# Cross attention in a decoder layer: where the head outputs are divided by their softmax sums

## The reference

```
x = x + self_attention(layernorm(x))                 # 2 x 256 tokens, width 128, 16 heads of 64
x = x + cross_attention(layernorm(x), ctx, ctx, mask) # 16 heads of 8, 512 keys
x = x + ffn(layernorm(x))                             # shared expert and 8 experts, best 2 of 8
```

## Time and profile before

| what | us |
| --- | --- |
| median of 3 runs | 205.86 (205.72 to 267.74) |
| the profiled execution | 205.74 |
| span of its profile, first to last instruction | 203.9 |
| TensorE busy in the span | 192.7 (94%) |
| VectorE busy | 157.2 (77%) |
| ScalarE busy | 138.0 (68%) |
| GpSimd busy | 96.6 (47%) |

### The profile page before, as it was taken

The page is one execution under the profiler, slowest core; times in us unless marked ns, Lnnn a source line. Parts: engine busy times, 40 slices in busy tenths (PEclk is TensorE's granted clock), DMA queues, the critical chain, the costliest instruction groups (busy, mean ns, idle before and its releaser), DMA issues.

```text
span 203.9 us, 4609 instructions
## 1 busy us (share of the span) xinstructions
PE 192.7 (94%) x1626; PEld 151.2 (74%) x1626; DVE 157.2 (77%) x418; ACT 138.0 (68%) x318; POOL 96.6 (47%) x145
## 2 busy tenths in 40 slices
PE   7999998999999699996999999999989999999995
PEld 7688776777877467764666657575568799999994
DVE  2579989668868677679999999999973866458844
ACT  2599879669766939189998898987986332452220
POOL 7599127588458835806669991003300017500430
PEclk9999999999999889999999999999999999999999
DMA  6970407604555015579844100000000000000001
GB/s 159 385 217 3 154 2 244 225 2 59 59 62 58 2 39 119 73 90 119 94 117 111 21 2 0 5 0 3 0 0 3 5 0 0 3 0 13 3 0 39
DMA packets 13301, 12.69 MB, mean 62 GB/s; under 512 B 1072, under 2 KB 11312, under 8 KB 13280
## 3 DMA queue, kind: packets, MB, share of 16 engines
q1 hardware_dynamic: 12176, 11.15, 26.7%
q10 hardware_dynamic: 1008, 1.06, 1.6%
q0 software_dynamic: 96, 0.20, 0.5%
HBM read 10.96 MB, written 1.44 MB: 61 GB/s over the span
## 4 chain that ended last, share of the span: by engine, by line
PE 75%; DVE 9%; ACT 7%; issue 3%; POOL 2%; DMA 1%; DVEq 0%; POOLq 0%
PE ps L985 13%; PE ps L944 9%; PE ps L886 8%; PE ps L870 8%; PE ps L1009 8%; PE ps L754 6%; PE ps L921 5%; PE ps L842 5%; PE ps L903 4%; PE ps L767 4%; ACT q_t L669 3%; ACT prob L635 2%; DVE q_t L1215 2%; DMA x_in<-in_x 1%; DVE prob_t L1323 1%
## 5 line engine op out<-in xcount | busy, mean ns | idle before, releaser
L509 POOL TENSOR_TENSOR prob<-prob,rec 128x512 f32<-128x512 f32 x32 | 32.7, 1047 | 24.2 <-DVE rec L1274 24.2
L1215 DVE CUSTOM_DVE_ANT_0 q_t<-ps,mask_add 128x512 f32<-128x512 f32 x64 | 41.4, 685 | 3.4 <-PE ps L903 2.2
L635 ACT ACTIVATE prob<-ps,low 128x256 f32<-128x256 f32 x64 | 29.7, 489 | 7.3 <-DVE low L1205 7.3
L669 ACT ACTIVATE q_t<-q_t,low 128x512 f32<-128x512 f32 x44 | 29.4, 719 | 4.2 <-DVE low L1215 4.1
L944 PEld LDWEIGHTS ps<-ident,q_t 128*128 128x128 f32 x176 | 19.6, 141 | 8.7 <-ACT q_t L669 2.9
L1205 DVE TENSOR_REDUCE low<-ps 128x2 f32<-128x512 f32 x32 | 20.5, 684 | 7.2 <-PE ps L842 7.1
L944 PE MATMUL ps<-ident,q_t 128*128 128x128 f32 x176 | 23.7, 276 | 2.1 <-ACT place_k L707 0.8
L548 POOL TENSOR_TENSOR place_k<-place_k 128x256 f32<-128x256 f32 x10 | 7.3, 733 | 38.7 <-DVE place_k L1240 38.7
L655 ACT ACTIVATE q_t<-ps 128x512 f32<-128x512 f32 x18 | 10.6, 599 | 21.1 <-PE ps L985 21.0
L886 PE MATMUL ps<-ident,prob 128*128 128x128 f32 x128 | 19.0, 283 | 2.7 <-ACT prob_t L643 1.4
L1261 DVE TENSOR_TENSOR q_t<-q_t,ps 128x512 f32<-128x512 f32 x18 | 12.2, 684 | 11.4 <-PE ps L985 8.2
(11 more groups left out here) (183 smaller groups left out, 470.7 us busy)
## 6 DMA issues: line engine op xcount, KB each, us to landing
k_stack<-k_dram SPq DMA_DIRECT2D x18, 128.0 KB
wg<-in_L_ffn_w_gate SPq DMA_DIRECT2D x1, 1024.0 KB, 5.4
wu<-in_L_ffn_w_up SPq DMA_DIRECT2D x1, 1024.0 KB, 8.0
q_stack<-q_dram SPq DMA_DIRECT2D x6, 144.0 KB
k_dram<-prob SPq DMA_DIRECT2D x1, 768.0 KB, 3.6
w_in<-in_L_attn_Wq ACTq DMA_DIRECT2D x2, 256.0 KB, 5.5
context<-in_ctx SPq DMA_DIRECT2D x1, 512.0 KB, 5.7
w_in<-in_L_attn_Wv SPq DMA_DIRECT2D x1, 512.0 KB, 7.3
```

The source lines that it names most:

```text
L509: nc.gpsimd.tensor_tensor(pr, pr, rec1[:, s % 2, r, :].unsqueeze(2).to_broadcast([P, C, S]), ALU.mult).then_inc(s_norm1, 1)
L635: e = nc.scalar.activation(prob1[:, s % 3, r, c * S:(c + 1) * S], ps[:, 2 * (s % 2) + r, c * S:(c + 1) * S], ACT.Exp, bias=low1[:, s % 2, ...
L669: nc.scalar.activation(prob2[n % 3][:, c, :], score2[n % 2][:, c, :], ACT.Exp, bias=low2[:, n % 2, c:c + 1], scale=-1.0).then_inc(s_exp2, 1)
L1215: nc.vector.tensor_tensor_reduce(out=score2[n % 2][:, c, :], in0=ps[:, 2 * (n % 2) + c, :], in1=mask_add[:, c, :], scale=1.0, scalar=3e38, ...
```

## The change

VectorE no longer divides. ScalarE copies the transposed outputs with their sums (72 of the 256 columns) out of PSUM to `o_sum` in SBUF, between `exp2(n)` and the copy of the second half of `turn2(n-2)`. GpSimd raises the sums to the power -1 and multiplies. `values2(k+1)` now waits for ScalarE's copy (`s_osum`) and no longer for the division.

```diff
+        o_sum = sb("o_sum", [P, C, HG, HD2 + 1])
+        minus_one = sb("minus_one", [P, C, HG])
...
             link(nc.gpsimd.memset(minus_half[:, :], -0.5))
+            nc.gpsimd.memset(minus_one[:, :, :], -1.0)
...
@@ GpSimd, step n, after the norms, before split_weights
+                if n in O_READY:
+                    k = O_READY[n]
+                    b, hg = divmod(k, NG)
+                    pool.wait_ge(s_osum, k + 1)
+                    link(nc.gpsimd.tensor_tensor(rec2[:, :, :], o_sum[:, :, :, HD2], minus_one[:, :, :], ALU.pow))
+                    nc.gpsimd.tensor_tensor(
+                        o2[:, b * C:(b + 1) * C, hg * HG * HD2:(hg + 1) * HG * HD2].rearrange("p c (g d) -> p c g d", g=HG),
+                        o_sum[:, :, :, 0:HD2], rec2[:, :, :].unsqueeze(3).to_broadcast([P, C, HG, HD2]), ALU.mult
+                        ).then_inc(s_o2, 1)
                 if 0 <= n - SPLIT_N < 2 * (NE + 1):
                     split_weights(n - SPLIT_N)
@@ ScalarE, step n
                 if 0 <= n < N_CROSS:
                     exp2(n)
+                if n in O_READY:
+                    k = O_READY[n]
+                    act.wait_ge(s_oturn, k + 1)
+                    if k >= 1:
+                        act.wait_ge(s_o2, k)
+                    nc.scalar.copy(o_sum[:, :, :, :], ps[:, O2_BANK[k], S:2 * S].rearrange(
+                        "p (c g d) -> p c g d", c=C, g=HG)[:, :, :, 0:HD2 + 1]).then_inc(s_osum, 1)
@@ TensorE, values2
-                        pe.wait_ge(s_o2, k)
+                        pe.wait_ge(s_osum, k)
@@ VectorE, step n
-                if n in O_READY:
-
-                    k = O_READY[n]
-                    b, hg = divmod(k, NG)
-                    dve.wait_ge(s_oturn, k + 1)
-                    o = ps[:, O2_BANK[k], S:2 * S].rearrange("p (c g d) -> p c g d", c=C, g=HG)
-                    link(nc.vector.reciprocal(rec2[:, :, :], o[:, :, :, HD2]))
-                    nc.vector.tensor_tensor(
-                        o2[:, b * C:(b + 1) * C, hg * HG * HD2:(hg + 1) * HG * HD2].rearrange("p c (g d) -> p c g d", g=HG),
-                        o[:, :, :, 0:HD2], rec2[:, :, :].unsqueeze(3).to_broadcast([P, C, HG, HD2]), ALU.mult
-                        ).then_inc(s_o2, 1)
```

More of the change, by code:

```diff
@@ L324, in build @@
         s_turn2a, s_turn2b, s_pt2a, s_pt2b = map(sem, ("s_turn2a", "s_turn2b", "s_pt2a", "s_pt2b"))
-        s_pv2, s_oraw, s_oturn, s_o2 = map(sem, ("s_pv2", "s_oraw", "s_oturn", "s_o2"))
+        s_pv2, s_oraw, s_oturn, s_osum, s_o2 = map(sem, ("s_pv2", "s_oraw", "s_oturn", "s_osum", "s_o2"))
         s_o2turn, s_o2t = map(sem, ("s_o2turn", "s_o2t"))
```

## The result

The changed kernel takes 208.17 us in the median of 17 executions (205.91 to 209.81), the kernel before 204.88 in the median of 17 (204.04 to 309.72), so the medians differ by 3.29 us. The ratio is 1.0105 with a 95% interval of 1.0077 to 1.0133, 2.15 us more; it leaves out slow executions, those more than 1.5% above the fastest of their kernel, which are five of the changed kernel's (209.35 to 209.81, granted clock 0.982 to 0.984). The forecast was 207.8 us in a range of 206.0 to 209.6, and +2.0 us on the kernel before.

What follows compares the result with a forecast made beforehand. It took TensorE, VectorE and ScalarE as nearly equally full, in periods of 8.11 us. The terms 0 + 1.99 + 0 - 0.38 + 0 + 0.41 gave +2.0 us on 205.74, a median of 207.8, range 206.0 to 209.6.

Steps and rivals of the forecast that it cites:

- Part 2: Step 23, turn_o2(0) waiting for group 3: copy, power, product and hand-overs start it 1.99 us later (1.0 to 2.6).
- Part 4: Groups 6 and 7 beside the first experts: 0 for group 6, +0.41 us for group 7 before turn_o2(1).
- Part 3: Groups 4 and 5, steps 26 and 30: 0 for group 4, -0.38 us for group 5 from VectorE's relief.
- Part 1: Regular periods of groups 0 to 2: ScalarE's new copy uses up VectorE's relief of 0.43 us; three periods 0 us (-0.3 to +0.6).
- its loop: Chain of steps through ScalarE in one regular period: 7.89 us plus the new copy's 0.17 to 0.23, giving 8.06 to 8.12.
- third rival: Regular periods and step 30: VectorE's relief passes whole, each period 0.43 us shorter, together -1.7, time 205.2; chance 0.07.
- the flat power: GpSimd's power costs 0.72 us per instruction whatever its size: +0.6 us in all, 206.5; chance 0.22.
- the factor of two: GpSimd's power and product cost twice VectorE's time, 0.86 us in all: +0.4 us, 206.3; chance 0.06.
- the full relief: Regular periods and step 30: ScalarE's idle time absorbs the copy, VectorE's relief passes whole, 205.2 us; chance 0.07.
- the ScalarE bound: ScalarE's copy of 0.37 us adds 0.2 per regular period and the power takes 2.3 us: +4.1, 210.0; chance 0.10.

Runs made afterwards that it cites:

- e8: The changed kernel with GpSimd's power split into two linked instructions of 128x4 instead of one of 128x8; 209.54 us in one execution, with a fall of the granted clock.
- e5: The kernel before without any division: VectorE's two instructions per group left out, consumers waiting for the turned outputs; 203.16 us, ratio 0.9933.
- e2: The changed kernel with groups 3 and 7 divided by VectorE out of PSUM as before, without ScalarE's copy for them; 204.25 us, ratio 0.9952.
- e9: The changed kernel with groups 3, 6 and 7 divided by VectorE and ScalarE's copy for the others behind the second-half copy; 203.88 us, ratio 0.9956.
- e4: The changed kernel with turn_o2(0) and what follows from it for the first batch one step later; 204.68 us, ratio 0.9964.
- e11: The changed kernel itself run again, unaltered, to look at its granted clock; 208.06 us, ratio 1.0137 against the kernel before.

## Why the prediction was right

Part 2, the wait at step 23, was the step that carried the sum, and it held: +1.84 against +1.99. Its terms measured: copy ready 0.42, copy 0.22 (0.23), power 1.64 (1.70), product 0.30 (0.33), three hand-overs 0.20 (0.25), together 2.78. The slope between the powers over two and four elements was the right reading, and e8 confirms it. The factor-of-two rule of the Trainium skill (GPSIMD Engine Reference, "Performance versus the Vector engine") doesn't cover a power: 1646 ns against VectorE's reciprocal of 206 is eight times. For the product over 128x64 the ratio is 1.3, 297 ns against 224.

Part 4 held for group 7, +0.35 against +0.41, and for the slack of group 6: the SiLU pair slid as forecast, from 0.67 us after group 6's turn to 2.44 us after it (156.68 to 159.12), and TensorE didn't wait: the interval to group 7 grew by 0.05. One sign was off there: ScalarE's idle time before its copies for groups 6 and 7 was 2.25 and 2.33 us, not about 1. Part 3 held: -0.01 and -0.44.

Part 1 came near the measured periods, 8.06 to 8.12 against 8.00, but by luck: its loop isn't in the rows. It counts "copy 0.52, o_raw 0.27" between two pairs of exponentials, where the trace has 0.58 us and no o_raw:

```profile
126.27 0.56 ACT L707 COPY prob<-ps 128x512 f32<-128x512 f32 x1
126.85 1.34 ACT L669 ACTIVATE place_k<-q_t,low 128x512 f32<-128x512 f32 x2
```

The o_raw copies stand at 122.32 and 130.43, and the new copy stands before the second-half copy at 123.83, not before the one at 128.09, where the loop has it. Without both, and with 0.58, the steps add up to 7.68. What holds the period above that is TensorE's own work, 7.86 (e5), which the prediction names only against its third rival, as "some 0.2 us per period". The 0.21 us too much in the loop stood where that limit should have stood. The new copy does cost time, 0.14 us per period, but through the copy behind it, for which TensorE's transposes wait. That 7.89 and the copy's hold of 0.11 also add up to 8.00 is chance. The three periods gave -0.34, just outside the -0.3 to +0.6 of this part. The copy's hold was forecast from the spacing of a longer copy before exponentials; in front of another copy out of PSUM it is shorter.

What the forecast did not have is the granted clock after the wait, and the 0.27 us outside the span, which it held at 1.84. By the profile alone the change costs 1.52 us, and by the executions at full clock 1.67, against +2.0. The absolute time came nearer to the measured 208.17 than its reasons entitle it to. The base of 205.86 was the median of three executions and its profile had a fall of the clock, while over 17 the kernel before has 204.88; and more than half of the changed kernel's executions had a fall, which the forecast put at nothing. At full clock the changed kernel takes 206.21.

The rivals: the flat power is out by e8, the factor of two by the 1646 ns, the full relief by the periods (8.00 and not 7.68; even with no division 7.86), the ScalarE bound by the same 8.00, for it needed periods of 8.3.

## What to carry to other kernels

When work moves off a busy engine, list its consumers first: here six of the eight divisions had time to spare and two were waited for at once, and a 1.65 us power on GpSimd, free for six groups, was most of TensorE's loss for one (1.43 of 1.84 us). Which consumers wait at once is read from the timeline of the step in which each stands. Either leave the awaited ones where they were (e2, e9) or put a step of other work between producer and consumer (e4). In a loop where three engines are nearly full, taking work off one gains only up to the next limit (0.25 of 0.43 us here, then TensorE), and the place of a small copy in a queue counts for more than its length: 0.14 us per period in front of the copy that the next engine waits for, 0 behind it.

## What was not expected of the hardware

An elementwise power on GpSimd took 719, 1010 and 1646 ns for 2, 4 and 8 elements of a row, by estimate 0.16 us per element and 0.4 fixed, so that at eight elements it takes eight times VectorE's reciprocal (206 ns), while a product over the same 128x8 took 206 ns.

An idle wait of TensorE (1.96 us in e11, 2.41 in e8) in the middle of a busy stretch was followed, in these two profiles, by over 3 us at a granted clock of 0.50, which added 1.5 us to the wait's own cost. In the first profile of the changed kernel a wait of 1.97 us was followed by none.
